# The last stages of a software-pipelined transformer network, in another order on all engines: an output projection split over two stages, transposed P in q's PSUM banks, a last FFN in three banks, gates spread on ScalarE

## What is computed

```python
for i in range(6):                                   # DEPTH, x is (4 x 512, 128) here
    x = attn_layer(shift_tokens(x), Wqkv[i], q_scale[i], k_scale[i], Wo[i]) + x
    x = ffn_layer(shift_tokens(x), ln_g[i], ln_b[i], W1[i], b1[i], W2[i], b2[i]) + x
# attn_layer: qkv = x @ Wqkv; 16 heads of 64, q and k normed and rotated,
#   softmax over a window of 32 keys and the 32 before it, out @ Wo
# ffn_layer: layernorm, hg = xn @ W1 + b1; a, gate = split(hg); a * gelu(gate) @ W2 + b2
# then, for the next layer:
x = x0 + s * silu(g)
xn = layernorm(x)
```

## Time and profile before

| | |
|---|---|
| median of 3 runs | 1829.21 us (1826.84 to 1832.83) |
| span of the profiled execution, first to last instruction | 1822.0 us |
| time of the profiled execution outside its span | not recorded; the median is 7.2 us above the span |
| TensorE busy | 1755.0 us, 96% |
| VectorE busy | 1454.4 us, 80% |
| ScalarE busy | 1162.8 us, 64% |
| GpSimd busy | 1190.7 us, 65% |
| mean granted TensorE clock | 0.986 |
| network's last stages without a tile of their own, to the end of its block | about 1665 to 1722.3 us |

### The profile page before, as it was taken

The page is one execution under the profiler, slowest core; times in us unless marked ns, Lnnn a source line. Parts: engine busy times, 40 slices in busy tenths (PEclk is TensorE's granted clock), DMA queues, the critical chain, the costliest instruction groups (busy, mean ns, idle before and its releaser), DMA issues. The chain is left out here.

```text
span 1822.0 us, 70687 instructions
## 1 busy us (share of the span) xinstructions
PE 1755.0 (96%) x30348; PEld 1136.7 (62%) x30348; DVE 1454.4 (80%) x1677; ACT 1162.8 (64%) x2032; POOL 1190.7 (65%) x1285
## 2 busy tenths in 40 slices
PE   7988999999999999999999999999999999998788
PEld 6855665665666566566666666656656656665466
DVE  6488789888788888888868978888887887896485
ACT  4356667667666765766766766676576676675644
POOL 1059678787677777767767867777776777775000
PEclk9899999999999999999999999999999999999999
DMA  4023222323222333223223223223223232222031
GB/s 151 1 50 77 58 72 66 92 66 80 73 68 68 95 78 73 73 57 98 73 67 80 68 64 98 67 69 80 72 60 91 70 81 69 65 68 74 1 71 47
DMA packets 87669, 128.94 MB, mean 71 GB/s; under 512 B 26776, under 2 KB 32800, under 8 KB 87360
## 3 DMA queue, kind: packets, MB, share of 16 engines
q1 hardware_dynamic: 87360, 124.43, 26.6%
HBM read 25.70 MB, written 1.11 MB: 15 GB/s over the span
## 5 line engine op out<-in xcount | busy, mean ns | idle before, releaser
L488 POOL TENSOR_TENSOR lent<-t,lent 128x1024 f32<-128x1024 f32 x192 | 455.2, 2371 | 356.7 <-DVE lent L955 356.6
L479 POOL TENSOR_TENSOR lent<-lent,rn 128x512 f32<-128x512 f32 x384 | 400.7, 1075 | 13.8
L619 PEld LDWEIGHTS sc_ps<-shared,v_win 64*64 64x64 f32 x12288 | 198.0, 135 | 147.1 <-issue 146.1
L791 ACT ACTIVATE sq<-qk_ps 128x1024 f32<-128x1024 f32 x192 | 196.1, 1021 | 94.9 <-PE qk_ps L556 94.2
L571 PEld LDWEIGHTS ring<-ident,lent 128*128 128x128 f32 x1536 | 176.5, 141 | 118.5 <-issue 76.8
L571 PE MATMUL ring<-ident,lent 128*128 128x128 f32 x1536 | 241.7, 280 | 5.7 <-POOL lent L479 5.3
L496 POOL TENSOR_TENSOR shared<-shared,rden 128x512 f32<-128x512 f32 x192 | 196.4, 1044 | 68.8 <-DVE rden L939 68.8
L784 ACT COPY shared<-ring 128x512 f32<-128x512 f32 x192 | 111.3, 580 | 198.2 <-PE ring L603 197.5
L955 DVE TENSOR_TENSOR lent<-qk_ps,rot 128x1024 f32<-128x1024 f32 x192 | 232.5, 1211 | 0.0
L965 DVE TENSOR_REDUCE sums<-sq 128x16 f32<-128x1024 f32 x192 | 231.7, 1207 | 0.0
L951 DVE TENSOR_TENSOR t<-qk_ps,rot 128x1024 f32<-128x1024 f32 x192 | 229.2, 1194 | 1.9 <-ACT sq L791 1.8
(11 more groups left out here) (213 smaller groups left out, 2736.4 us busy)
## 6 DMA issues: line engine op xcount, KB each, us to landing
v_win<-v_tok SPq DMA_DIRECT2D x1488, 64.0 KB, 2.0
wqkv<-in_w_qkv SPq DMA_DIRECT2D x18, 512.0 KB, 3.7
spread<-gate_rows SPq DMA_DIRECT2D x32, 128.0 KB, 3.7
wo<-in_w_o SPq DMA_DIRECT2D x6, 512.0 KB, 3.8
w<-in_w SPq DMA_DIRECT2D x6, 341.0 KB, 3.3
w<-in_w SPq DMA_DIRECT2D x6, 192.0 KB, 3.0
r_xtok<-in_x SPq DMA_DIRECT2D x4, 256.0 KB, 3.9
out_x<-xo SPq DMA_DIRECT2D x4, 256.0 KB, 2.3
```

The lines of the kernel that those rows point to most:

```text
L479: nc.gpsimd.tensor_tensor(by_head(quarter(qkn, f)), by_head(quarter(qkn, f)), rn[:, 8 * f:8 * (f + 1)].unsqueeze(2).to_broadcast([P, 8, DH ...
L488: nc.gpsimd.tensor_tensor(half(qkn, k), half(t1, k), half(t2, k), ALU.add).then_inc((q_added, k_added)[k], 1)
L619: ins = nc.tensor.matmul(sc_ps[64 * par:64 * (par + 1), part, P * pair + WIN * q:P * pair + WIN * (q + 1)], v_win[64 * part:64 * (part + 1 ...
```

## The change

- Half 0 of round 23's output projection is done in stage 97 (it was in 98 with half 1), behind the down product of round 22, and both stand ahead of `attend(94)`.
- P of tile 95 is transposed into q's banks, `qk_ps` 0 and 1, and no longer into the ring.
- In round 23 the second gate product and the third lin product go to the score bank `sc_ps` 1.
- `ffn_down` waits for u by chunk, in all rounds.
- silu of batch 0 and 1 is in stage 97, of batch 2 in stage 98 (all were in 98). VectorE's gated products of batches 0 and 1 are written ahead of half 1's addition in stage 98's place.
- Deviation of batch 0 moves to stage 99; a second load of Gelu's table is gone. Variance of batch 1 moves to stage 99, variance of batch 2 to stage 101. The square of batch 2 moves behind the gelus, `normed` of batch 0 ahead of them, `normed` of 1 and 2 behind `add_ffn`.

```diff
+        LAST = ROUNDS - 1
+        def first_half_of(g):
+            r = round_at(g, 2, 1)
+            return LAST if g == TILE_COUNT + 1 else r if r != LAST else None
...
-        place = {f: n for n, f in enumerate(all_fills)}
+        p_home = [("p", TILE_COUNT - 1, f) for f in range(2)]
+        third_home = [("gate", LAST, 1), ("lin", LAST, 2)]
+        in_ring = [f for f in all_fills if f not in p_home and f not in third_home]
+        homes = {f: (ring[:, n % 2, :], in_ring[n - 2] if n >= 2 else None) for n, f in enumerate(in_ring)}
+        homes.update({f: (qk_ps[:, n, :], None) for n, f in enumerate(p_home)})
+        homes.update({f: (sc_ps[:, 1, :], third_home[0] if n else None) for n, f in enumerate(third_home)})
...
             def ffn_down(r):
-                pe.wait_ge(u_ready, 3 * (r + 1))
                 to = ring_bank("w2", r, 0)
                 for c, m in enumerate(FCH):
+                    pe.wait_ge(u_ready, 3 * r + c + 1)
                     ins = nc.tensor.matmul(to, w2[0:m, c, :], gel[0:m, c, :], start=(c == 0), stop=(c == 2))
...
+                if g == TILE_COUNT + 1:
+                    ffn_down(down)
+                    output_projection(out_0, 0)
                 if tile_there(g - 3):
                     attend(g - 3, 0)
...
                     norm.variance(pe, 0, qk_ps[:, 3, :], mean_w)
-                if g == TILE_COUNT + 4:
-
                     pe.wait_ge(oT_copied, 2 * TILE_COUNT)
                     norm.variance(pe, 1, sc_ps[:, 0, :], mean_w)
-                    norm.variance(pe, 2, sc_ps[:, 1, :], mean_w)
+                if g == TILE_COUNT + 5:
+                    pe.wait_ge(norm.logs, 1)
+                    norm.variance(pe, 2, qk_ps[:, 3, :], mean_w)
...
+                if g == TILE_COUNT + 1:
+                    act.wait_ge(x_ffn, 2 * (ROUNDS - 2))
+                    norm.silu(act, 1)
...
-                if g == TILE_COUNT + 3:
+                if g == TILE_COUNT + 2:
                     norm.gated_x1(dve, 0)
                     norm.gated_x1(dve, 1)
...
+                if g == TILE_COUNT + 5:
                     norm.normed(dve, 1, qk_ps[:, 1, :])
                     norm.normed(dve, 2, qk_ps[:, 2, :])
-                if down is not None:
-                    add_ffn(down)
```

More of the change, by code:

```diff
@@ L389, in build_network @@
         all_fills = [f for g in range(STAGES) for f in stage_fills(g)]
-        place = {f: n for n, f in enumerate(all_fills)}
+        p_home = [("p", TILE_COUNT - 1, f) for f in range(2)]
[4 more added lines that the diff above has]
+        homes.update({f: (sc_ps[:, 1, :], third_home[0] if n else None) for n, f in enumerate(third_home)})
         def bank_of(*fill):
-            return ring[:, place[fill] % 2, :]
+            return homes[fill][0]
         def bank_free(*fill):
-            n = place[fill] - 2
-            if n < 0:
+            before = homes[fill][1]
+            if before is None:
                 return None
-            what, of, f = all_fills[n]
+            what, of, f = before
             return dict(t=(qkT_copied, 4 * of + turn_at.get(f, 0) + 1), v=(v_copied, 2 * of + f + 1), p=(pT_copied, 2 * of + f + 1),
@@ L599, in transpose_p @@
                 pe.wait_ge(p_scaled, 2 * g + f + 1)
+                if g == TILE_COUNT - 1 and f == 0:
+                    pe.wait_ge(q_sq, TILE_COUNT)
+                    pe.wait_ge(q_rot, 2 * TILE_COUNT)
                 to = ring_bank("p", g, f)
@@ L649, in ffn_up @@
                     pe.wait_ge(xn_ready, r + 1)
+                if c == 1 and r == LAST:
+                    pe.wait_ge(oT_copied, 2 * TILE_COUNT)
                 nc.tensor.matmul(ring_bank("gate", r, c)[0:m, :], w1[:, FF + P * c:FF + P * c + m], xn[:, :],
@@ L662, in _ @@
             for g in range(STAGES):
-                out_0 = round_at(g, 2, 1)
+                out_0 = first_half_of(g)
                 out_1 = round_at(g, 2, 1)
@@ L708, in _ @@
                     transpose_qk(g - 1, 0)
-                if down is not None:
+                if down is not None and g != TILE_COUNT + 1:
                     ffn_down(down)
@@ L722, in _ @@
                     ffn_up(up, 2)
-                if out_0 is not None:
+                if out_0 is not None and g != TILE_COUNT + 1:
                     output_projection(out_0, 0)
@@ L849, in _ @@
                     exponentials(g - 2, 1)
+                if g == TILE_COUNT + 1:
+                    act.wait_ge(q_added, TILE_COUNT)
+                    act.wait_ge(k_added, TILE_COUNT)
+                    act.wait_ge(x_ffn, 2 * (ROUNDS - 3))
+                    norm.silu(act, 0)
                 if up is not None:
-                    nc.scalar.preload_act_table_set(GELU_SET)
+                    if up != LAST:
+                        nc.scalar.preload_act_table_set(GELU_SET)
                     gelu(up, 0)
@@ L868, in _ @@
                     act.wait_ge(x_ffn, 2 * (ROUNDS - 1))
[L869 to L872, removed]
+                    norm.silu(act, 2)
                     nc.scalar.preload_act_table_set(LN_EXP_SET)
@@ L877, in _ @@
                 if g == TILE_COUNT + 4:
-                    norm.deviation(act, 0, qk_ps[:, 3, :], eps_col)
+                    norm.square(act, 2, qk_ps[:, 2, :])
                     norm.deviation(act, 1, sc_ps[:, 0, :], eps_col)
-                    norm.deviation(act, 2, sc_ps[:, 1, :], eps_col)
+                    norm.deviation(act, 2, qk_ps[:, 3, :], eps_col)
                 if centre is not None:
@@ L892, in _ @@
                 if g == TILE_COUNT + 3:
+                    norm.deviation(act, 0, qk_ps[:, 3, :], eps_col)
                     nc.scalar.preload_act_table_set(GELU_SET)
-                    norm.square(act, 2, qk_ps[:, 2, :])
                 if tile_there(g - 2):
                     copy_pT(g - 2, 1)
+                if g == TILE_COUNT + 1:
+                    act.wait_ge(x_ffn, 2 * (ROUNDS - 2))
+                    norm.silu(act, 1)
         @block.vector
@@ L1015, in _ @@
                     ffn_norm(spread)
+                if g == TILE_COUNT + 4:
+                    norm.normed(dve, 0, qk_ps[:, 0, :])
                 if g == 1:
@@ L1040, in _ @@
                     ffn_gated(up, 2)
-                if g == TILE_COUNT + 4:
-                    norm.normed(dve, 0, qk_ps[:, 0, :])
+                if down is not None:
+                    add_ffn(down)
+                if g == TILE_COUNT + 5:
                     norm.normed(dve, 1, qk_ps[:, 1, :])
                     norm.normed(dve, 2, qk_ps[:, 2, :])
-                if down is not None:
-                    add_ffn(down)
                 if out_0 is not None:
```

4 lines of the change are left out of this document (1 added, 3 removed).

## The result

| | before | changed |
|---|---|---|
| median of 8 runs | 1830.28 us (1824.09 to 1833.55) | 1818.98 us (1811.18 to 1826.12) |
| ratio | | 0.994, 95% interval 0.9919 to 0.9961 |
| span of the profiled execution | 1822.0 us | 1818.0 us |
| T0, VectorE's masking of the last tile's scores | 1676.90 us | 1683.64 us |
| T0 to the centring matmul | 25.3 us | 18.7 us |

The account below looks back on a forecast made before the run. TensorE was taken to bound the whole execution, but the last stages to be a chain of waits. Part one's 6.3 us and part two's 2.6 us summed to 8.9 us, giving 1820.3 us, range 1816 to 1826.

Parts of the forecast that it names:

- Down(22) and the first half in the gap: Stage 97: both fill TensorE's idle 3.41 us; attention of tile 94 starts 2.7 us later, but needs 2.0 us.
- part one: Stages 97 to 99, the edits up to the projection's second half: gain 6.3 us, all priced at 2.4 GHz.
- Its term for the split: Last projection: its first half out of the way, 3.6 us, less copies of 1.1 us that it used to hide.
- No bank to wait for, P in q's banks: Transposes of the last P start at 1685.55 with no bank to wait for; before, they waited 1.28 us.
- Silu(1) with 0.9 us of cover: ScalarE: silu(1) ends at 1689.1, next copy due 1690.0, so it costs nothing; placed later, up to 1.3 us.
- Part two: Stages 99 to 102: down product 2.9 us earlier, third variance then last; the block's end gains 2.6 us.
- Rival 2: The block's end doesn't follow the down product: part two worth 0.5 us or so, gain 6.8, 1822.4 us; chance 0.12.
- The clock in the thinned stretch: Stages 97 to 99: clock kept at 1.00 despite waits of about 1.3, 1.1 and 1.2 us between 1686.6 and 1695.9.
- Rival 1: The clock falls in the thinned stretch, giving away up to 3.3 us: gain 5.6, time 1823.6 us; chance 0.14.
- The waits in each round: The 23 rounds before: 46 added waits taken as nothing, upper bound 3.7 us; rival of a slower kernel, chance 0.03.
- rival 4: Second layer's restart: the gap ahead shrinks to 3.7 us; if the clock is kept, some 2 us more, 1818.3; chance 0.08.
- 7.2 us lie outside the span: Whole execution: trace of 1822.0 us against a median of 1829.21, so 7.2 us are added to turn span into time.

Follow-up runs that it names:

- experiment 1: The changed kernel with the last projection's first half back in stage 98, the down product still early: ratio 0.996 to the kernel before, centring at T0+19.66.
- experiment 2: The changed kernel with the projection's first half and the down product both back behind attention of tile 94: ratio 0.9969 to the kernel before, centring at T0+23.76.
- experiment 5: The changed kernel with P of tile 95 transposed into the ring again: ratio 0.9946 to the kernel before, centring at T0+18.71.
- experiment 8: The changed kernel with two more half silus, read by nobody, behind silu(1) on ScalarE: ratio 0.9953 to the kernel before, centring at T0+18.86.
- experiment 6: The changed kernel with all three silus in stage 98 again, behind the copies of tile 95's attention: ratio 0.9971 to the kernel before, centring at T0+20.37.
- experiment 4: The changed kernel with each of the down product's three waits for u written eleven times, in all 24 rounds: 1820.61 us, ratio 0.9962 to the kernel before.
- experiment 3: The changed kernel with stages 99 to 102 as before: ratio 0.9963 to the kernel before, one execution of 3420.98 us left out; centring at T0+18.71.
- experiment 7: The changed kernel with the last FFN's products all in the ring's two banks: ratio 0.994 to the kernel before, block's end at T0+37.21.
- the last session: The session in which the changed kernel was measured once more, unaltered: 1821.02 us, ratio 0.9954 to the kernel before.
- experiment 9: The changed kernel with two more matmuls behind the last variance, ahead of the second layer: ratio 0.9943 to the kernel before, second layer's stretch 98.3 us.
- experiment 10: The kernel of experiment 9 with three more such matmuls in the second layer's attention bank: 1818.23 us, ratio 0.994 to the kernel before, second layer's stretch 97.1 us.

## Why the prediction was right, step by step

Since T0 differs, I set each step against the changed kernel's trace from T0 (T0 was 1676.90 in the forecast's clock).

- **Down(22) and the first half in the gap**: forecast to start at T0+0.4, attention of tile 94 at +6.65; measured +0.39 and +6.52. Right. Experiments 1 and 2 show the down product's move to be the larger part of part one, 4.1 of 6.6 us, and 3.3 of these to be the clock. The sum has this gain in it, since it priced the attention at 2.4 GHz. Its term for the split, 3.6 less 1.1 us, is not what the split is worth: in experiment 1 it is 2.2 us from the attention of tile 95 to the centring, less the 1.24 by which the first half holds that attention up, 0.95 net.
- **No bank to wait for, P in q's banks**: right that there was no wait, but it is no gain of its own. In the ring the banks would have been free 0.6 to 1.1 us earlier than needed (experiment 5). The wait of 1.28 us in the earlier trace rows goes with either move: with the down product's in experiment 5, with P in q's banks in experiment 2.
- **Silu(1) with 0.9 us of cover**: measured 0.90, and shown by experiment 8; the need to spread the silus at all by experiment 6.
- **Attention of tile 95** at T0+11.0 forecast, +10.76 measured; the centring at +19.0, measured +18.71. The term was 6.3 us and measured 6.58.
- **Part two**: first gelu 8.1 us behind the centring, measured 1710.47 - 1702.35 = 8.12; down product 11.7 (11.72); gain 2.6 us, measured 2.65. The third variance is indeed what ends last, but only just: its Exp ends at 1719.06, and VectorE, with the addition and the normalisation of batch 1 ahead of it, comes to its normalisation at 1719.09. Rival 2 did not happen.
- **The clock in the thinned stretch**: stayed at 1.00, in TensorE busy 5.84 of 9.1 us. Rival 1 did not happen, here or in any of the traces with both moves, by their attention of tile 95 (2.07 us in each). That idleness lets the clock fall, as the Trainium skill has it ("TensorE: Matmul & The Clock Gate", Part 1), experiment 2 shows again, but waits of 1.1 to 1.2 us did not call it up.
- **The waits in each round** cost nothing that can be measured (experiment 4); in the traces of before and of the changed kernel the additions of FFN to state of eight rounds in a row, from 972 to 1432 us, stay 4.2 to 4.3 us apart, where a cost in each round would add up.
- **The restart (rival 4)**: partly so. It ran two passes in 1.44 us, and the layer behind it took 98.2 us instead of 99.7, a gain of 1.5 that I had at 2 with a chance of 0.08. But the same stretch took 98.1 to 99.8 us in the kernels of experiments 1, 2, 3, 5, 6, 7 and 8, whose second layer is the same, and 95.9 in experiment 4. So the 1.5 us can't be put down to the change.

What was wrong is the step from span to time: "7.2 us lie outside the span". The eight runs of the changed kernel have 1.8 to 2.1 us between span and time (1819.96 and 1818.0 in the profiled one), and the 70 of the kernel before in the three sessions of experiments 1.7 to 2.2. The 1822.0 us span of before therefore belonged to an execution of about 1824 us (the quickest of the 8 of its kernel took 1824.09). The missing 5 us are probably a slower way to T0 in the median run, which has no trace. It did no harm, since only the difference of spans was carried over to the median.

The account: 6.6 + 2.65 = 9.2 us shown in the traces, 0 to 1.5 us in the second layer, which is luck where it is there at all. The measured 11 us has an interval of 7 to 15, and 8.4 us (0.9954) came out in the last session. The rest is not resolved.

## What to carry to other kernels

In a drained pipeline look for the long wait of the engine on the chain and for work of its own queue that is ready by then: the cheapest move here, one line's place, brought 4.1 of 9.2 us, about 0.8 by filling a wait and 3.3 by the clock that was kept. When the piece that used to hide other engines' work gets shorter, what it hid must be spread before the next waits, with its cover checked in tenths of a microsecond. And where runs spread by 0.5% for reasons ahead of the change, measure from an event right ahead of it: in seven traces whose T0 lie 10.8 us apart (the changed kernel's two and experiments 3, 5, 7, 9 and 10) the centring came at the same distance from T0 to 0.01 us.

## What I had not expected of the hardware

- The way to T0, the same program but for added waits (and, before, for two waits fewer a round), took from 1676.9 to 1691.8 us over 13 traces, while from T0 to the block's end the changed kernel's two traces agree to 0.01 us. Between the traces of before and of the changed kernel the rounds' additions of FFN drift apart by 6 us from 768 to 904 us, stay about 4 us apart from 972 to 1630 us, and go to 6.7 us in the last stretch before T0, where the changed kernel's trace has its low clock. What sets these steps off I did not find.
- Idleness of TensorE ahead of the second layer of 3.66 us or of 1.95 us ended in the low clock all the same, at the restart or a microsecond behind it (experiments 4 and 9 for the latter). It stayed away in one trace, the one with further waits filled (experiment 10). In the same kernels waits of 1.15 and 1.19 us with 2.07 and 3.72 us of work between them left it at 1.00.
